# Two-layer gated attention block: the second layer's query projection, groups 2 to 6, by seven block products in place of eight

## The chip, the cores and the metric

The kernel runs on one core of a Trainium2 chip. The metric is the device time of one execution in microseconds (us), as the median of several runs of the same kernel. The engines are TensorE (PE: matmuls; PEld: its weight loads), VectorE (DVE), ScalarE (ACT), GpSimd (POOL) and SyncE (SP, which here only issues transfers). Each engine works through its own list of instructions in order, and the lists are tied together by semaphores.

## What is computed

The input is 16 sequences of 64 tokens with 512 features (1024 tokens in all), a context of the same shape, and two layers. Each layer is a gated attention over the context followed by a gated feed-forward part. The change touches the attention of the second layer alone, in the reference's own words:

```python
def _L1_xattn_ref(hidden_states, cross_attention_states, attention_mask, Wq, Wk, Wv, Wo, q_norm_w, k_norm_w):
    H, KVH, HD = (32, 8, 128)
    q = (hidden_states @ Wq.T).reshape(bsz, q_len, H, HD).transpose(0, 2, 1, 3)
    k = (cross_attention_states @ Wk.T).reshape(bsz, kv_len, KVH, HD).transpose(0, 2, 1, 3)
    v = (cross_attention_states @ Wv.T).reshape(bsz, kv_len, KVH, HD).transpose(0, 2, 1, 3)
    q = _rmsnorm(q, q_norm_w)
    k = _rmsnorm(jnp.repeat(k, GROUPS, axis=1), k_norm_w)
    scores = jnp.einsum('bhqd,bhkd->bhqk', q, k) * scale + attention_mask
    probs = jax.nn.softmax(scores.astype(jnp.float32), axis=-1)
    out = jnp.einsum('bhqk,bhkd->bhqd', probs, jnp.repeat(v, GROUPS, axis=1))
    return out.transpose(0, 2, 1, 3).reshape(bsz, q_len, H * HD) @ Wo.T
```

Everything is float32. A product of two float32 matrices is made of three passes on TensorE (`three`, L224): each operand is split into a high part of a shorter type (`_hi`, made by ScalarE) and the rest (`_lo`, made by a subtraction), and high x high, high x low and low x high are summed.

## The kernel before

The 32 query heads form 8 groups of 4 heads (J = 4); a group shares one key and value head. The 1024 tokens are cut into two halves of 512 (HALF). A unit u = 2g + h is one group g on one half h. The attention runs in steps, one for each unit, by a list written out by hand for each engine (`att_steps`, L881): groups 0, 1 and 7 are written out, groups 2 to 6 are a loop. Step (g, h) does three things at a time, for three units: the query projection of unit u, the scores and the softmax of unit u - 1, and values and output projection of unit u - 2.

TensorE's part of a step of the second layer (`step` in `att_pe`, L1022): the 16 small score matmuls of unit u - 1 (`score`, L966), which wait for the folded squares of its queries; the sums of squares for the norm (`folded_sums`, L947); `values` of unit u - 2 (L982), which waits for both parts of the probabilities (`p_hi`, `p_lo`) and for the last output addition of unit u - 3 (`y_added`), since it writes the same banks; then four heads of `project` (L924), 12 matmuls of 512 columns each, and four tiles of `project_out` (L1010), 12 matmuls of 512 columns each. The first `project` waits for `ssq_t`, that is until VectorE has read the sums out of PSUM; the score matmuls of the next step wait until VectorE has read the scores (`s_turned`).

VectorE's part (`step` in `att_dve`, L1532), in its order: `turn_sums` (L1439: two transposes out of PSUM, then eight copies of 32x16 elements, L1457, which end in `ssq_all`), `turn_scores` (L1432), `scale_scores` (L1473), the mask (L791), `maxima` (L1488 to L1496), two `out_low` (L1514: low parts of the values' output), `fold_squares` (L1463) for two heads, two `out_low`, `sums` (L1500, ends in `p_rec`), two `add_output` (L1521: adds a tile of the output projection to x), `turn_probs` (L1508), `fold_squares` for the other two heads, `att_probs_low` (L808: p_lo), two `add_output`.

GpSimd's part (`step` in `att_pool`, L1319): `att_shift` (L797, subtracts the maxima), `att_normalise` (L803), the low parts of the output weights (`wo_low`, L1310, four in a step h = 0) and of the next group's query weights (`att_wq_low`, L743, four in a step h = 1). In a step h = 0 the second, third and fourth `wo_low` are held back until `ssq_all`:

```python
                    for j in wo if do_finish and h == 0 and not (isinstance(g, int) and g == 1) else ():
                        if lay and j == 1:
                            pool.wait_ge(*c("ssq_all", us + 1))
                        wo_low(g - 1, j)
```

ScalarE squares and copies each head of queries out of PSUM (`queries`, L1144), makes the high parts, the exponentials and the norm factors (`norms`, L1155, from `ssq_all`). SyncE loads weights a group ahead. In group 1 the step (1, 0) is special (`second_opening`): VectorE does the shift itself there.

## Time and profile before

| | us |
|---|---|
| median of 3 runs | 1179.5 (1179.32 to 1179.86) |
| time of the profiled execution | 1179.01 |
| its span, first to last instruction | 1177.1 |
| one step of the loop of the second layer | 26.07 |
| second layer's attention, first scores to the last query step | about 746 to 1102 |

The page gives for each engine the busy share of the span, then the span in slices, the chain that ended last, and the costliest groups of instructions. Matmuls are pipelined: the duration of one is longer than the distance to the next, so TensorE's price is read from the distances between starts in the timeline, and not from the durations. On the other engines a duration includes the time in which an instruction has started but is held up.

### The profile page before, as it was taken

How to read it: one execution, taken by the hardware profiler on the slowest of the kernel's cores; microseconds unless marked ns; L12 is line 12 of the kernel's file. 1: busy time of each engine (PE TensorE's matmuls, PEld its weight loads, DVE VectorE, ACT ScalarE, POOL GpSimd, SP SyncE). 2: the span in 40 equal slices, each digit the busy share in tenths (PEclk: the TensorE clock that was granted, in tenths of full speed). 3: DMA queues.
4: the chain of work that ended last, by engine and by line, in shares of the span. 5: the costliest groups of instructions: out<-in, count | busy, mean ns of one | idle time of the engine just before them, and what ended most of it. 6: DMA issues, size and time to landing. Idle time of an engine off the chain costs nothing.

```text
span 1177.1 us, 17132 instructions
## 1 busy us (share of the span) xinstructions
PE 1169.5 (99%) x6272; PEld 946.7 (80%) x6272; DVE 880.9 (75%) x1538; ACT 424.0 (36%) x748; POOL 532.9 (45%) x371
## 2 busy tenths in 40 slices
PE   9999999999999999999999999999999999999998
PEld 8888888888788888777788888777777777777776
DVE  4656646898888888889984335798888887888695
ACT  5145152322322222231552123535453443435542
POOL 5522533766667676677463112305242433425410
PEclk9999999999999999999999999999999999999999
DMA  7944735812211221211210003121221221121101
GB/s 286 285 137 159 211 111 162 287 55 81 81 66 59 89 80 45 80 45 45 99 64 36 1 1 107 55 94 57 91 80 45 80 80 54 71 89 39 43 1 72
DMA packets 57315, 106.54 MB, mean 91 GB/s; under 512 B 3633, under 2 KB 36529, under 8 KB 51889
## 3 DMA queue, kind: packets, MB, share of 16 engines
q1 hardware_dynamic: 56736, 104.82, 26.0%
q0 software_dynamic: 384, 1.05, 0.2%
q8 instruction: 32, 0.52, 0.2%
q14 instruction: 19, 0.15, 0.0%
q10 hardware_dynamic: 144, 0.00, 0.0%
HBM read 78.59 MB, written 27.26 MB: 90 GB/s over the span
## 4 chain that ended last, share of the span: by engine, by line
PE 96%; DVE 2%; issue 0%; ACT 0%; DVEq 0%; POOL 0%; POOLq 0%
PE ps_q L226 14%; PE ps_b L226 14%; PE ps_b L228 14%; PE ps_b L227 14%; PE ps_q L227 13%; PE ps_q L228 13%; PE ps_s L978 5%; PE ps_b L1005 4%; PE ps_s L278 1%; PE ps_q L953 1%; PE ps_q L2152 1%; PE ps_b L479 1%; PE ps_s L1847 1%; PE ps_q L529 0%; PE ps_b L529 0%
## 5 line engine op out<-in xcount | busy, mean ns | idle before, releaser
L226 PE MATMUL ps_q<-hT_hi,wq_hi 128*128 128x512 f32 x512 | 203.2, 397 | 0.0
L227 PE MATMUL ps_q<-hT_lo,wq_hi 128*128 128x512 f32 x512 | 199.6, 390 | 0.0
L228 PE MATMUL ps_q<-hT_hi,wq_lo 128*128 128x512 f32 x512 | 199.2, 389 | 0.0
L226 PE MATMUL ps_b<-wo_hi,o_hi 128*128 128x512 f32 x440 | 171.6, 390 | 0.0
L227 PE MATMUL ps_b<-wo_lo,o_hi 128*128 128x512 f32 x440 | 171.2, 389 | 0.0
L228 PE MATMUL ps_b<-wo_hi,o_lo 128*128 128x512 f32 x440 | 171.2, 389 | 0.0
L743 POOL TENSOR_TENSOR wq_lo<-wq_raw,wq_hi 128x512 fp32r<-128x512 f32 x64 | 90.2, 1413 | 112.8 <-ACT wq_hi L737 112.8
L1317 POOL TENSOR_TENSOR qT<-q_t 128x512 f32<-128x512 f32 x64 | 89.8, 1405 | 66.3 <-DVE q_t L1430 60.8
L226 PEld LDWEIGHTS ps_q<-hT_hi,wq_hi 128*128 128x128 f32 x512 | 96.1, 188 | 24.3 <-issue 1.5
L228 PEld LDWEIGHTS ps_q<-hT_hi,wq_lo 128*128 128x128 f32 x512 | 96.1, 188 | 20.3
L227 PEld LDWEIGHTS ps_q<-hT_lo,wq_hi 128*128 128x128 f32 x512 | 96.2, 188 | 18.7
L1310 POOL TENSOR_TENSOR wo_lo<-wo_raw,wo_hi 128x512 fp32r<-128x512 f32 x56 | 83.5, 1507 | 56.4 <-ACT wo_hi L1142 38.3
L1184 ACT ACTIVATE p_hi<-pT 128x1024 fp32r<-128x1024 f32 x32 | 34.0, 1061 | 189.7 <-DVE pT L1512 189.7
L226 PEld LDWEIGHTS ps_b<-wo_hi,o_hi 128*128 128x128 f32 x440 | 82.6, 188 | 18.4 <-issue 1.4
L228 PEld LDWEIGHTS ps_b<-wo_hi,o_lo 128*128 128x128 f32 x440 | 82.6, 188 | 17.1
L227 PEld LDWEIGHTS ps_b<-wo_lo,o_hi 128*128 128x128 f32 x440 | 82.6, 188 | 17.1
L1529 DVE SCALAR_TENSOR_TENSOR x_sb<-ps_b,gates,x_sb 128x512 f32<-128x512 f32 x115 | 81.4, 722 | 18.0 <-PE ps_b L228 17.5
L803 POOL TENSOR_TENSOR p_sb<-p_sb,p_rec 128x1024 f32<-128x1024 f32 x29 | 55.7, 1920 | 83.8 <-DVE p_rec L1506 83.8
L1518 DVE TENSOR_TENSOR o_lo<-ps_b,o_hi 128x512 fp32r<-128x512 f32 x128 | 81.8, 682 | 12.6 <-ACT o_hi L1191 10.7
L1191 ACT ACTIVATE o_hi<-ps_b 128x512 fp32r<-128x512 f32 x128 | 66.5, 607 | 34.0 <-PE ps_b L1005 26.7
L1177 ACT ACTIVATE p_sb<-s_sb,zero_b 128x1024 f32<-128x1024 f32 x32 | 37.2, 1162 | 96.9 <-POOL s_sb L797 93.5
L797 POOL TENSOR_TENSOR s_sb<-s_sb,mx_c 128x1024 f32<-128x1024 f32 x28 | 53.8, 1921 | 32.1 <-DVE mx_c L1485 32.1
(301 smaller groups left out, 2498.0 us busy)
## 6 DMA issues: line engine op xcount, KB each, us to landing
wq_raw<-in_wq SPq DMA_DIRECT2D x16, 1024.0 KB, 4.8
...
```

The source lines that it names most:

```text
L226: nc.tensor.matmul(dst, l_hi, r_hi, start=first, stop=False)
L227: nc.tensor.matmul(dst, l_hi, r_lo, start=False, stop=False)
L228: return nc.tensor.matmul(dst, l_lo, r_hi, start=False, stop=last)
L743: nc.gpsimd.tensor_tensor(wq_lo[:, :, j * D:(j + 1) * D], wq_raw[:, :, j * D:(j + 1) * D], wq_hi[:, :, j * D:(j + 1) * D].bitcast(F32), AL ...
L797: eng.tensor_tensor(sc, sc, wide(mx_c[:, :], QB), ALU.subtract).then_inc(c["s_shifted"], 1)
L803: eng.tensor_tensor(pr, pr, wide(p_rec[:, :], QB), ALU.mult).then_inc(c["p_normed"], 1)
L978: last = nc.tensor.matmul(ps_s[par * S:(par + 1) * S, t * JS:(t + 1) * JS], kT[:, h, b:b + S], qT[:, h, :, b:b + S], start=True, stop=True)
L1191: nc.scalar.activation(o_hi[:, 2 * half:2 * half + 2, :, par * S:(par + 1) * S], ps_b[n].rearrange("p (t j q) -> p t j q", t=2, j=J), ACT. ...
L1310: nc.gpsimd.tensor_tensor(lo, wo_raw[:, j, :], hi.bitcast(F32), ALU.subtract).then_inc(c["wo_lo"], 1)
L1317: nc.gpsimd.tensor_tensor(qT[:, h, j, :], q_t1[:, j % 2, :], q_t2[:, j % 2, :], ALU.add).then_inc(c["q_rot"], 1)
L1518: nc.vector.tensor_tensor(o_lo[part], ps_b[n].rearrange("p (t j q) -> p t j q", t=2, j=J), o_hi[part].bitcast(F32), ALU.subtract).then_inc ...
L1529: nc.vector.scalar_tensor_tensor(x_sb[:, i, :], out_bank(u, t)[:, :], gates[:, lay:lay + 1], x_sb[:, i, :], ALU.mult, ALU.add).then_inc(c[ ...
```

## The change

For groups 2 to 6 of the second layer (ten units) the query projection of a unit, a product of a weight block of 512 features by 512 outputs with 512 tokens, is taken as a 2x2 by 2x2 product of blocks of 256 and made of seven block products in place of eight (the Strassen form of Winograd). A block product is 12 matmuls of 256 columns (2 output heads, 2 feature tiles, 3 passes), so a unit's projection is 84 matmuls of 256 columns in place of 48 of 512.

- The mixed token blocks t1 to t4 are made once for all groups by GpSimd, in the steps (0, 1), (1, 0) and (1, 1), with high parts by ScalarE and low parts by GpSimd: six instructions of 128x1024 after `lora_center` in (0, 1) and at the start of (1, 0), two after `att_normalise` in (1, 0), two at the start of (1, 1), four low parts.
- The mixed weight blocks s1 to s4 are made for each group by GpSimd (four sums of 128x512); each group then needs seven high parts (ScalarE) and seven low parts (GpSimd) of 128x512 in place of four and four. Six of the seven low parts stand behind `att_normalise` of the step h = 1; the four `wo_low` of the next step follow them, with no wait for `ssq_all`.
- Partial products that serve two outputs are joined by VectorE (four additions of 128x512 with one operand in PSUM for each unit), by two copies on ScalarE and by one addition on GpSimd. TensorE waits in between for two copies (`copied`) and for a join (`joined`), and its third product waits for `s_turned` as it writes the bank of the scores.
- `fold_squares` becomes two instructions of 64x1024 in place of four of 64x512. `turn_sums` stays as it is: VectorE still copies the sums of squares. The factor `qk_w` moves from the query copies to the staging of the keys, and its load to the start. Group 6 is written out after the loop, buffers are placed anew, some semaphore increments are dropped, and the scratch of software DMAs is set to 2048.

```diff
-                                 ACT.Copy).then_inc(c["k_staged1"], 1)
+                                 ACT.Copy, scale=qk_w[:, 0:1]).then_inc(c["k_staged1"], 1)
...
+        def woven(lay, g):
+            return lay == 1 and not (isinstance(g, int) and g in (0, 1, G - 1))
+        def builds_woven(lay, g, next_wq):
+            return lay == 1 and next_wq and not (isinstance(g, int) and g in (0, G - 2))
...
+        WOVEN_PARTS = ("a11", "s2", "s3", "a12", "a22", "s1", "s4")
...
+        def woven_low(pool, gt, name):
+            c = att[1]
+            pool.wait_ge(*c("woven_hi", 7 * (gt - 2) + WOVEN_PARTS.index(name) + 1))
+            f, hi, lo = woven_parts(name)
+            nc.gpsimd.tensor_tensor(lo, f, hi.bitcast(F32), ALU.subtract).then_inc(c["woven_lo"], 1)
...
+                l, r = woven_parts("s1")[0], woven_parts("a11")[0]
...
+                l, r = woven_parts("a22")[0], s2_f[:, :, :]
...
+                l, r = woven_parts("a12")[0], s2_f[:, :, :]
+            nc.gpsimd.tensor_tensor(out, l, r, ALU.subtract).then_inc(c["s_f"], 1)
...
+                    for q in range(2):
+                        for k in range(2):
+                            col = slice(q * D, (q + 1) * D)
+                            dst, closes = bank[:, q * QT:(q + 1) * QT], last_one and (q, k) == (1, 1)
+                            nc.tensor.matmul(dst, l_hi[:, k, col], r_hi[:, k, :], start=first and (q, k) == (0, 0), stop=False, skip_group_check=True)
+                            nc.tensor.matmul(dst, l_hi[:, k, col], r_lo[:, k, :], start=False, stop=False, skip_group_check=True)
+                            last = nc.tensor.matmul(dst, l_lo[:, k, col], r_hi[:, k, :], start=False, stop=closes, skip_group_check=True)
+                    return last
...
+                pe.wait_ge(*c("ssq_t", u))
+                if h == 0:
+                    pe.wait_ge(*c("t_hi", 4))
+                    pe.wait_ge(*c("t_lo", 4))
+                product(ps_q[0], "a11", tokens(0, 0), True).then_inc(c["product"], 1)
+                product(ps_q[1], "s2", mixed(t2_hi, t2_lo), True, True).then_inc(c["product"], 1)
+                pe.wait_ge(*c("s_turned", u))
+                product(ps_h[0], "s3", mixed(t3_hi, t3_lo), True).then_inc(c["product"], 1)
+                pe.wait_ge(*c("copied", 2 * n + 1))
+                product(ps_q[0], "a12", tokens(1, 0), False, True).then_inc(c["q_done"], 1)
+                product(ps_h[1], "s1", mixed(t1_hi, t1_lo), True).then_inc(c["q_done"], 1)
+                pe.wait_ge(*c("joined", 4 * n + 2))
+                product(ps_h[0], "a22", mixed(t4_hi, t4_lo), False, True).then_inc(c["q_done"], 1)
+                pe.wait_ge(*c("copied", 2 * n + 2))
+                product(ps_h[1], "s4", tokens(1, 1), False, True).then_inc(c["q_done"], 1)
...
+            def woven_step(g, h, next_wq):
...
+                norms(us)
+                act.wait_ge(*c("product", 3 * n + 1))
+                act.wait_ge(*c("scored", u - 1))
+                nc.scalar.activation(qT[:, h, 0:2, late], heads(ps_q[0]), ACT.Copy).then_inc(c["copied"], 1)
+                out_high(up, 0)
+                out_high(up, 1)
+                if building:
+                    woven_high(act, g + 1, "a11")
+                out_high(up, 2)
+                out_high(up, 3)
+                if building:
+                    woven_high(act, g + 1, "s2")
+                act.wait_ge(*c("q_done", 4 * u + 1))
+                act.wait_ge(*c("ssq", u))
+                nc.scalar.activation(q_sq[:, 0:2, early], heads(ps_q[0]), ACT.Square).then_inc(c["q_sq"], 1)
+                nc.scalar.activation(qT[:, h, 0:2, early], heads(ps_q[0]), ACT.Copy).then_inc(c["q_rot"], J)
+                act.wait_ge(*c("q_done", 4 * u + 2))
+                nc.scalar.activation(q_sq[:, 2:4, late], heads(ps_h[1]), ACT.Copy).then_inc(c["copied"], 1)
+                if building:
+                    woven_high(act, g + 1, "s3")
+                exponentials(us)
+                act.wait_ge(*c("joined", 4 * n + 3))
+                square(slice(2, 4), early)
+                if building:
+                    woven_high(act, g + 1, "a12")
+                elif next_wq:
+                    att_wq_high(act, lay, g + 1, 0)
+                act.wait_ge(*c("joined", 4 * n + 4))
+                square(slice(0, 2), late)
+                act.wait_ge(*c("c22_made", n + 1))
+                square(slice(2, 4), late)
+                if building:
+                    woven_high(act, g + 1, "a22")
+                    woven_high(act, g + 1, "s1")
+                    woven_high(act, g + 1, "s4")
+                elif next_wq:
+                    for j in range(1, J):
+                        att_wq_high(act, lay, g + 1, j)
+                probs_high(us)
...
+                if second_opening(lay, g, h):
+                    mixed_high(t1_hi, t1_f, 3)
+                    mixed_high(t2_hi, t2_f, 8)
...
+            def mixed_first(f, t, l, r):
+                pool.wait_ge(*lns[2]("lo", NT))
+                nc.gpsimd.tensor_tensor(by_half(f), quarters(hT_hi, *l), quarters(hT_hi, *r), ALU.subtract).then_inc(c["t_f"], 1)
+                nc.gpsimd.tensor_tensor(by_half(t), quarters(hT_lo, *l), quarters(hT_lo, *r), ALU.subtract).then_inc(c["t_f"], 1)
+            def mixed_joined(f, t, turn):
+                pool.wait_ge(*c("t_f", turn - 1))
+                nc.gpsimd.tensor_tensor(f[:, :, :], f[:, :, :], t[:, :, :], ALU.add).then_inc(c["t_f"], 1)
+            def mixed_next(f, l, r, turn, before):
+                pool.wait_ge(*c("t_f", before))
+                nc.gpsimd.tensor_tensor(by_half(f), quarters(hT_hi, *l), by_half(r), ALU.subtract).then_inc(c["t_f"], 1)
+                pool.wait_ge(*c("t_f", turn - 1))
+                nc.gpsimd.tensor_tensor(by_half(f), by_half(f), quarters(hT_lo, *l), ALU.add).then_inc(c["t_f"], 1)
+            def mixed_low(lo, hi, f, turn):
+                pool.wait_ge(*c("t_hi", turn))
+                nc.gpsimd.tensor_tensor(lo[:, :, :], f[:, :, :], hi[:, :, :].bitcast(F32), ALU.subtract).then_inc(c["t_lo"], 1)
...
+            def woven_step(g, h, next_wq):
...
+                if h == 0:
+                    for j in range(J):
+                        wo_low(g - 1, j)
+                elif building:
+                    woven_sum(pool, g + 1, "s2")
+                    woven_sum(pool, g + 1, "s3")
+                    woven_low(pool, g + 1, "a11")
+                att_shift(pool, lay, u - 1)
+                pool.wait_ge(*c("copied", 2 * n + 2))
+                pool.wait_ge(*c("joined", 4 * n + 2))
+                nc.gpsimd.tensor_tensor(qT[:, h, 2:4, late], qT[:, h, 2:4, late], q_sq[:, 2:4, late], ALU.add).then_inc(c["c22_made"], 1)
+                if h and building:
+                    woven_sum(pool, g + 1, "s4")
+                elif next_wq:
+                    att_wq_low(pool, lay, g + 1, 0)
+                att_normalise(pool, lay, u - 1)
+                if h == 0 and not (isinstance(g, int) and g == G - 2):
+                    woven_sum_first(pool, g + 1)
+                elif building:
+                    for name in WOVEN_PARTS[1:]:
+                        woven_low(pool, g + 1, name)
+                elif next_wq:
+                    for j in range(1, J):
+                        att_wq_low(pool, lay, g + 1, j)
...
+                if second_opening(lay, g, h):
+                    mixed_joined(t3_f, t3_t, 6)
+                    att_normalise(pool, lay, us)
+                    mixed_next(t2_f, (1, 1), t1_f, 8, 3)
+                    woven_sum_first(pool, 2)
+                    woven_sum(pool, 2, "s2")
+                    woven_sum(pool, 2, "s3")
+                    woven_sum(pool, 2, "s4")
+                    mixed_low(t1_lo, t1_hi, t1_f, 1)
+                    return
+                if builds_woven(lay, g, next_wq):
+                    mixed_next(t4_f, (1, 0), t2_f, 10, 8)
+                    att_shift(pool, lay, us)
+                    mixed_low(t2_lo, t2_hi, t2_f, 2)
+                    woven_low(pool, 2, "a11")
+                    woven_low(pool, 2, "s2")
+                    att_normalise(pool, lay, us)
+                    woven_low(pool, 2, "s3")
+                    woven_low(pool, 2, "a12")
+                    mixed_low(t3_lo, t3_hi, t3_f, 3)
+                    woven_low(pool, 2, "a22")
+                    woven_low(pool, 2, "s1")
+                    mixed_low(t4_lo, t4_hi, t4_f, 4)
+                    woven_low(pool, 2, "s4")
...
+                    mixed_first(t1_f, t1_t, (0, 1), (0, 0))
+                    mixed_joined(t1_f, t1_t, 3)
+                    mixed_first(t3_f, t3_t, (1, 1), (0, 1))
...
+                dve.wait_ge(*c("q_sq", 4 * u + 2 * r + 2))
+                nc.vector.tensor_tensor(q_sq[own, :, tok], q_sq[own, :, tok], q_sq[other, :, tok], ALU.add).then_inc(c["q_fold"], 2)
...
+            def woven_step(g, h):
...
+                turn_sums(us, 1 - h)
+                turn_scores(us, 1 - h)
+                scale_scores(us)
+                dve.wait_ge(*c("copied", 2 * n + 1))
+                dve.wait_ge(*c("product", 3 * n + 2))
+                joined(part_b, ps_q[1], part_b).then_inc(c["joined"], 1)
+                att_mask(dve, lay, us, 1 - h)
+                dve.wait_ge(*c("joined", 4 * n + 1))
+                dve.wait_ge(*c("product", 3 * n + 3))
+                joined(part_d, ps_h[0], part_b).then_inc(c["joined"], 1)
+                maxima(us)
+                out_low(up, 0)
+                out_low(up, 1)
+                dve.wait_ge(*c("q_done", 4 * u + 3))
+                joined(qT[:, h, 2:4, early], ps_h[0], part_b).then_inc(c["joined"], 1)
+                out_low(up, 2)
+                dve.wait_ge(*c("q_done", 4 * u + 4))
+                joined(part_b, ps_h[1], part_b).then_inc(c["joined"], 1)
+                out_low(up, 3)
+                sums(us)
+                add_output(up, h, 0)
+                fold_woven(u, 0)
+                turn_probs(us)
+                fold_woven(u, 1)
+                att_probs_low(dve, lay, us)
+                for t in range(1, PAIRS):
+                    add_output(up, h, t)
...
```

## Rows read from the trace of the kernel before

**Rows 1.** The page: busy time of the engines; the chain that ended last, by engine.
```profile
PE 1169.5 (99%) x6272; PEld 946.7 (80%) x6272; DVE 880.9 (75%) x1538; ACT 424.0 (36%) x748; POOL 532.9 (45%) x371
...
PE 96%; DVE 2%; issue 0%; ACT 0%; DVEq 0%; POOL 0%; POOLq 0%
```
**Rows 2.** Timeline of TensorE, one step: start us, us, engine, line, what.
```profile
866.09 1.95 PE L978 MATMUL ps_s<-qT,kT 128*64 128x256 f32 x16
867.97 0.66 PE L953 MATMUL ps_q<-q_sq,ones 64*32 64x256 f32 x16
...
870.51 0.40 PE L227 MATMUL ps_q<-hT_lo,wq_hi 128*128 128x512 f32 x1
...
881.19 0.39 PE L226 MATMUL ps_b<-wo_hi,o_hi 128*128 128x512 f32 x1
...
892.16 1.95 PE L978 MATMUL ps_s<-qT,kT 128*64 128x256 f32 x16
```
**Rows 3.** Timelines of TensorE and of its weight loads: shorter matmuls elsewhere.
```profile
650.47 0.36 PE L227 MATMUL ps_b<-uT_lo,hT_hi 128*128 128x448 f32 x1
...
651.89 0.36 PE L228 MATMUL ps_b<-uT_hi,hT_lo 128*128 128x448 f32 x1
...
1152.35 1.75 PEld L2152 LDWEIGHTS ps_q<-a_raw,xT 128*128 128x128 f32 x15
```
**Rows 4.** Timeline of VectorE, the same step as rows 2.
```profile
869.64 1.43 DVE L1457 COPY r_s<-r_t 32x16 f32<-32x16 f32 x8
871.10 1.25 DVE L1435 STREAM_TRANSPOSE s_sb<-ps_s 128x1024 f32<-128x1024 f32 x1
872.45 1.23 DVE L1479 TENSOR_TENSOR s_sb<-s_sb,r_q 128x1024 f32<-128x1024 f32 x1
873.71 2.20 DVE L791 TENSOR_TENSOR s_sb<-s_sb,mask_sb 128x1024 f32<-128x1024 f32 x1
...
884.63 0.35 DVE L1506 RECIPROCAL p_rec<-sm_c 128x32 f32<-128x32 f32 x1
...
892.27 0.75 DVE L1529 SCALAR_TENSOR_TENSOR x_sb<-ps_b,gates,x_sb 128x512 f32<-128x512 f32 x1 [0.18 <-PE ps_b L228]
```
**Rows 5.** Timeline of GpSimd, the same step.
```profile
871.23 3.60 POOL L1310 TENSOR_TENSOR wo_lo<-wo_raw,wo_hi 128x512 fp32r<-128x512 f32 x2 [3.04 <-DVE r_s L1457]
...
885.06 1.92 POOL L803 TENSOR_TENSOR p_sb<-p_sb,p_rec 128x1024 f32<-128x1024 f32 x1 [5.08 <-DVE p_rec L1506]
```
**Rows 6.** Busy time by stretch, of step (1, 0); the first line names the columns.
```profile
core 0: us, PE busy (x) PEld busy (x) DVE busy (x) ACT busy (x) POOL busy (x), PEclk, DMA share, GB/s
761.30:787.70 26.40, 25.73 (x140) 20.39 (x137) 24.07 (x40) 10.65 (x19) 3.97 (x3) 1.00 0.23 90
```
**Rows 7.** VectorE's small instructions beside GpSimd: timelines at 747 and 280 us.
```profile
747.41 1.14 DVE L1457 COPY r_s<-r_t 32x16 f32<-32x16 f32 x2
747.07 1.27 POOL L1310 TENSOR_TENSOR wo_lo<-wo_raw,wo_hi 128x512 fp32r<-128x512 f32 x1 [2.38 <-ACT wo_hi L1142]
...
280.74 1.38 DVE L1485 TENSOR_TENSOR mx_c<-mx_a 32x32 f32<-32x32 f32 x2
280.79 1.29 POOL L1310 TENSOR_TENSOR wo_lo<-wo_raw,wo_hi 128x512 fp32r<-128x512 f32 x1
```
**Rows 8.** One line each, all its instructions: duration ns min/median/max.
```profile
L1457 DVE COPY r_s<-r_t x120: 161/167/946, 747.4 to 1103.9; 32x16 f32<-32x16 f32 x120
...
L1518 DVE TENSOR_TENSOR o_lo<-ps_b,o_hi x40: 678/686/694, 799.9 to 1038.4; 128x512 fp32r<-128x512 f32 x40
```
**Rows 9.** Timeline of VectorE and TensorE from step (1, 0) to (1, 1).
```profile
765.71 1.95 DVE L1457 COPY r_s<-r_t 32x16 f32<-32x16 f32 x8
...
773.32 1.29 DVE L1518 TENSOR_TENSOR o_lo<-ps_b,o_hi 128x512 fp32r<-128x512 f32 x2 [0.66 <-ACT o_hi L1191]
...
786.20 1.41 DVE L1470 TENSOR_TENSOR q_sq<-q_sq 64x512 f32<-64x512 f32 x2
...
787.71 1.95 PE L978 MATMUL ps_s<-qT,kT 128*64 128x256 f32 x16 [0.68 <-issue]
```

217 lines of the change are left out of this document (184 added, 33 removed).

## The prediction

> **What bounds the kernel now.** I read the page first: TensorE is busy 99% of the span and the chain that ended last lies on it for 96% [rows 1]. So the time is TensorE's own list, and each microsecond that its list gets shorter or longer is a microsecond of the kernel. Then the timeline of one step of the loop [rows 2]: the scores start at 866.09 and those of the next step at 892.16, so a step takes 26.07 us with no hole in it. From 870.51 to 881.19 lie 47 projection matmuls of 512 columns: 10.68/47 = 0.227 us from one to the next (durations of 0.39 overlap). Then VectorE in the same step [rows 4], since the change gives it work: it starts on the sums once they are there, at 868.63, that is T+2.5 (T is the start of the scores, 866.09) [rows 2], and its last instruction ends at 893.02, that is T+26.9, or 0.9 into the next step. It has to be clear of that by T+2.5 of the next step, where `values` writes the banks and the next sums are ready. So VectorE has some 1.6 us to spare in a step. GpSimd is busy for 4 of 26.4 us in the first such step [rows 6] and looks free.
>
> It is not free beside VectorE, and this decides the case. While GpSimd works on one `wo_low` after another, the scaling of the scores (872.45, 1.23 us) goes through, but the `wo_low` beside it stretches: two of them take 3.60 us where one takes 1.28 [rows 5, 7]. The mask behind it, the same size and also with both operands in SBUF, takes 2.20 instead of 1.23 [rows 4]. They exclude each other: each holds up the other for a whole instruction, and they take turns. Even the smallest are held: one copy of the sums has a median of 167 ns but a maximum of 946 [rows 8], and that one stands beside a `wo_low` (two copies in 1.14 us at 747.41) [rows 7]. At 280.74 two VectorE instructions of 180 ns take 1.38: the first passes, the second waits for GpSimd's whole instruction [rows 7]. Instructions that read PSUM are not held: `out_low`, one operand in PSUM, has a maximum of 694 over a median of 686, often with GpSimd busy beside it [rows 8]. The kernel before keeps clear of this where it hurts: GpSimd waits 3.04 us for the eighth copy before it goes on with `wo_low` [rows 5].
>
> The Trainium skill, page "SBUF — State Buffer", section "Who interferes with whom", says the same and speaks against the change: a VectorE instruction with two SBUF inputs contends with GpSimd's, a copy in a two-port mode does too, and whoever is first has the shared ports for its whole instruction. The trace agrees (2.20 against 1.23 us, 946 against 167 ns). By that rule the step below in which copies and GpSimd take turns holds, and the rival in which they don't falls.
>
> **The change on TensorE.** Per unit it removes 48 x 0.227 = 10.90 us and adds 84 matmuls of 256 columns. No full-height one of 256 columns is in the trace. The bounds: matmuls of 448 columns lie 1.42/7 = 0.203 us apart [rows 3], so 64 columns cost 0.024, and a straight line gives 0.227 - 4 x 0.024 = 0.131; by the 2.4 GHz level (clock 1.00 [rows 6]) 256 columns fewer are 0.107 less, 0.120. Weight loads of 128 columns follow each other every 1.56/14 = 0.111 us [rows 3], below that, so they stay hidden; if they did not, the sum of both, 0.23, would be the end. I take 0.121, from the clock. Saved: 10.90 - 84 x 0.121 = 0.73 a unit, 7.3 us in ten.
>
> The same skill's page "TensorE: Matmul & The Clock Gate", section "Back-to-back issue gap", gives N/2.4 + 2.5 ns for a matmul of N columns alone: 215.8 and 109.2 ns, and by it the saving would be 10.36 - 9.17 = 1.2 us a unit. The trace has 227 ns where the page has 216.
>
> **The change on VectorE and GpSimd.** VectorE gets four joins of 0.69 (the price of `out_low`, also one PSUM operand [rows 8]), + 2.5 us a unit as they start 0.62 apart. Four folds of 0.7 (1.41 for two [rows 9]) become two of 64x1024, for which I take the mask's 1.23 without wait [rows 4], - 0.3. GpSimd gets nine more instructions of 1.29 in a group (three low parts, four sums, two additions), 11.6 us. Prices: 1.29 for 128x512, 1.92 for 128x1024 [rows 5, 7]. I now walk through a group with these prices and the turn-taking.
>
> Second half (h = 1), T at its scores: copies T+3.4 to 4.8, scores read by 6.1, scaled by 7.3, first join 8.1; the mask waits for the s2 sum on GpSimd and ends at 9.8; maxima 12.8 (held 0.4 by a low part), two `out_low` by 14.1. TensorE's seven products, 1.45 us each from T+4.3, end at 14.4: no wait. `p_rec` at 18.9. Then GpSimd: normalise to 20.9, and six low parts and, from the next step, four `wo_low`, ten instructions 1.25 apart. VectorE's two folds and p_lo push in between, each waiting up to 1 us: folds 22.0 and 25.5, p_lo 27.7, and three output additions to 29.8. TensorE is done at T+25.5. GpSimd is done at 20.9 + 12.5 + 3 x 0.95 = 36.3.
>
> First half of the next group (h = 0), T at its scores, 25.5 later: VectorE comes free at 4.3 in place of 0.9, so `values` starts at 4.3 in place of 2.5 (1.8 lost), and the sums are transposed by 5.0. GpSimd has back-to-back work until 36.3 - 25.5 = 10.8. So one copy of 0.17 us passes between each two GpSimd instructions: 5.7, 6.9, 8.2, 9.4, and the other four from 10.7 to 11.4. The scores are read out by 12.7. TensorE's third product, which writes that bank, was due at 7.1 and starts at 12.7: 5.6 us lost in all. After it come four more products and the output projection, 5 x 1.45 + 10.97: the step ends at 30.9 against 26.07. GpSimd has little left to do by then, so the tail is free of waits: p_lo at 31.3, the additions at 33.4, that is T+2.5 of the next step, just in time.
>
> So groups 3 to 6: first half + 4.9 (four times, 19.5); second halves 25.5, - 0.55 (five times, - 2.8).
>
> Entry, step (1, 0) (T = 761.26, where T of the next is 26.45 later [rows 9]): GpSimd's six 128x1024 instructions run from T+5.7, while VectorE has done four of its eight copies. The other four each wait for one: 11.5 in place of 6.4. p_lo 14.4, scaling 17.3, mask 20.2, each behind another of them, so the two `out_low` end at 21.5 in place of 13.35 (774.61) [rows 9], and the output projection, due at 14.6, starts at 21.5. `p_rec` is at 29.7; after normalise (31.7) the two t2 instructions take turns with the folds, which end at 36.5 in place of 26.35 (787.61) [rows 9]. The next scores wait for them, as they already do today (0.68 us idle [rows 9]): + 10.0.
>
> Step (1, 1): ScalarE makes the high part of t2 before p_hi, so p_lo comes at T+3.5 and the additions at 4.9: `values` is 2.4 late. Copies take turns with s4, t1's low part and t4 (six us instead of 1.4), the two `out_low` are 2.0 late for the output projection, and the folds, behind low parts, end 3.4 after TensorE: + 7.8.
>
> First half of group 2: seven GpSimd instructions are left at the copies; the third product starts at T+13.2 in place of 7.1. It ends at 31.4: + 5.3.
>
> Sum: 10.0 + 7.8 + 5.3 + 19.5 - 2.8 = + 39.8 (TensorE's 7.3 saved is in it). The profiled execution is 1179.0 (1177.1 and 1.9 around); 1218.8, and as the median stands 0.5 above it, 1219.
>
> Edits priced at nothing: ScalarE's three more high parts a group (0.6 each; it is busy for 10.7 of 26.4 us [rows 6]); the key staging's factor (same instruction); the earlier load and the dropped increments. If the smaller DMA scratch slows the gathers at the start, it is some us, in no row.
>
> **The rivals.**
> - VectorE is served first when both ask. For it: the scaling at 872.45 went before a `wo_low` of 872.48. Against: the mask waited its turn. The walk then loses 3.3 us in a pair of steps less (27.8 for a first half), and less at the entry: + 20, 1199.
> - The small copies slip through together once GpSimd pauses. For: eight copies with one wait took 1.95 at 765.71 [rows 9]. Against: at 280.74 the second was held [rows 7], and GpSimd has no pause here. A first half then loses only 1.8 by late additions: 27.2, entry + 7 and + 5: + 14, 1193.
> - Heavier: joins are held too, or GpSimd's strided 128x1024 take 2.2: + 45, 1224.
> - The other side: the extra GpSimd work waits instead of VectorE, and TensorE stays the bound with - 7.3, of which the t2 chain before p_hi in (1, 1) gives back 3.3: 1175. It decides for faster if VectorE's waits stay under its 1.6 us to spare a step; the walk has 4 to 7. Against it: 946 ns for a copy of 167.
> - The block products cost 0.131 or show their weight loads: at 0.131, + 8.4 us of TensorE, part of it inside the waits, 1224; at 0.23, 84 x 0.11 x 10 = + 90.
>
> **Chances.** Forecast 0.50; VectorE first 0.15; copies pass 0.11; heavier 0.10; dearer matmuls 0.04; faster 0.07; about equal, by a mix of small waits, 0.03. The range that leaves out the last two and some of the dear end is 1190 to 1228. A measurement of this kernel can tell 0.2%, 2.4 us, from no change. Faster 0.07, within it 0.03, slower 0.90.
>
> **What the profile after would show.** The eight copies in a step h = 0 as one group of 6 to 7 us in place of 1.43; TensorE idle for about 3.7 us before the third product, released by VectorE's transposition of the scores; first halves of 31, second halves of 25.5; durations over 2 us for folds and p_lo; (1, 0) of 36 us. TensorE's matmuls of 256 columns 0.121 apart tell the price. The prediction is wrong if the copies stay at 1.4 us with GpSimd's instructions stretched instead, or if the chain stays on TensorE without holes.

## The result, and the profile after

The kernel after takes 1234.15 us (median of 5 runs, 1231.15 to 1235.16), the kernel before 1179.44 in the same session: 1.046 times as long, with a 95% interval from 1.0445 to 1.0474. The forecast was 1219 with a range up to 1228. The direction and most of the mechanism came out as worked out; the size did not, by 15 us, and the time lies outside the range.

The profiled execution has a span of 1233.3 us, 56.2 more than before. Its page: busy time of the engines, TensorE's busy share and granted clock in 40 slices, and the chain that ended last, by engine and by line:

```profile
PE 1178.6 (96%) x6632; PEld 968.6 (79%) x6632; DVE 965.7 (78%) x1558; ACT 429.0 (35%) x757; POOL 640.3 (52%) x430
...
PE   9999999999999999999999999687989898989998
...
PEclk9999999999999999999999999998999999999999
...
PE 19%; DVE 13%; issue 4%; POOL 1%; ACT 0%; DVEq 0%; ACTq 0%
DVE r_s L1777 3%; PE ps_b L252 3%; PE ps_b L254 3%; PE ps_b L253 3%; PE ps_s L1138 1%; PE ps_b L1165 1%; DVE o_lo L1845 1%; PE ps_s L1086 1%; DVE x_sb L1856 1%; DVE q_sq L1798 1%; PE ps_s L1088 1%; PE ps_s L1087 1%; PE ps_q L252 1%; DVE q_s
```

VectorE has 85 us more busy time than in [rows 1], of which 27 are the 40 joins. The chain no longer lies on TensorE for 96%: its share is 19% and VectorE's 13% (the shares printed add up to 37% only), and the copies of the sums (L1777) stand first in its list. TensorE's busy share is still 96%; its idle stretches, called holes here, show only as lower digits in the second half of the slices. The steps show them better. Busy time by stretch, steps (1, 0), (1, 1), (2, 0), (2, 1), (3, 0), (3, 1), each from one score to the next (columns as in [rows 6]: length, then busy time and instructions of TensorE, its weight loads, VectorE, ScalarE and GpSimd, then the clock and the DMA share and rate):

```profile
764.18:801.98 37.80, 27.77 (x140) 21.60 (x137) 36.06 (x39) 10.83 (x19) 26.57 (x12) 0.95 0.17 63
801.98:838.53 36.55, 28.34 (x152) 21.37 (x153) 33.50 (x39) 17.70 (x31) 28.42 (x16) 0.95 0.11 37
838.53:872.28 33.75, 28.97 (x188) 24.29 (x188) 31.05 (x41) 8.69 (x15) 18.98 (x12) 0.85 0.20 71
872.28:897.90 25.62, 25.44 (x189) 21.67 (x189) 23.95 (x40) 12.45 (x23) 15.85 (x10) 1.00 0.15 53
897.90:930.24 32.34, 26.97 (x188) 23.24 (x188) 30.73 (x42) 10.70 (x19) 17.89 (x12) 0.95 0.21 73
930.24:955.86 25.62, 25.39 (x189) 21.67 (x189) 23.94 (x40) 12.50 (x23) 15.87 (x10) 1.00 0.15 51
```

Three more pairs like the last follow (the last second half takes 25.13). The clock column is the one to look at: 1.00 in the second halves and below 1.00 wherever a step is long. The sums, in us against the kernel before (26.07 a step; 26.45 for (1, 0) [rows 9], 26.23 for (1, 1), 27.07 for (7, 0)):

| | forecast | measured | length |
|---|---|---|---|
| up to the first scores of the layer | 0 | + 2.9 | 749.4 |
| (1, 0) | + 10.0 | + 11.4 | 37.80 |
| (1, 1) | + 7.8 | + 10.3 | 36.55 |
| (2, 0) | + 5.3 | + 7.7 | 33.75 |
| four first halves, groups 3 to 6 | + 19.5 | + 25.1 | 32.3 each |
| five second halves | - 2.8 | - 2.9 | 25.6 to 25.1 |
| (7, 0), not woven | 0 | + 1.7 | 28.8 |
| sum | + 39.8 | + 56.2 | |

The first half (3, 0) line by line, with T = 897.90 at its scores. VectorE, timeline:

```profile
897.70 2.19 DVE L923 TENSOR_TENSOR p_lo<-pT,p_hi 128x1024 fp32r<-128x1024 f32 x1
899.82 2.06 DVE L1856 SCALAR_TENSOR_TENSOR x_sb<-ps_b,gates,x_sb 128x512 f32<-128x512 f32 x3
...
902.68 6.35 DVE L1777 COPY r_s<-r_t 32x16 f32<-32x16 f32 x8
909.06 1.25 DVE L1755 STREAM_TRANSPOSE s_sb<-ps_s 128x1024 f32<-128x1024 f32 x1
910.41 1.23 DVE L1806 TENSOR_TENSOR s_sb<-s_sb,r_q 128x1024 f32<-128x1024 f32 x1
```

GpSimd beside it, and then TensorE:

```profile
893.07 3.53 POOL L820 TENSOR_TENSOR s_lo<-s_f,s_hi 128x512 fp32r<-128x512 f32 x2
896.55 5.70 POOL L820 TENSOR_TENSOR wq_lo<-wq_raw,wq_hi 128x512 fp32r<-128x512 f32 x3
902.22 1.29 POOL L820 TENSOR_TENSOR s_lo<-s_f,s_hi 128x512 fp32r<-128x512 f32 x1
903.47 4.99 POOL L1546 TENSOR_TENSOR wo_lo<-wo_raw,wo_hi 128x512 fp32r<-128x512 f32 x4
```

```profile
901.92 0.39 PE L1165 MATMUL ps_b<-p_hi,v_hi 64*128 64x256 f32 x2 [1.48 <-DVE x_sb L1856]
...
906.26 0.28 PE L1087 MATMUL ps_q<-t_lo,s_hi 128*128 128x256 f32 x1
906.38 0.28 PE L1088 MATMUL ps_q<-t_hi,s_lo 128*128 128x256 f32 x1
910.55 0.36 PE L1086 MATMUL ps_s<-t_hi,s_hi 128*128 128x256 f32 x1 [3.88 <-DVE s_sb L1755]
...
911.49 0.41 PE L1086 MATMUL ps_s<-t_hi,s_hi 128*128 128x256 f32 x1
911.71 0.41 PE L1087 MATMUL ps_s<-t_lo,s_hi 128*128 128x256 f32 x1
...
914.26 0.41 PE L1087 MATMUL ps_q<-hT_lo,wq_hi 128*128 128x256 f32 x1
```

The eight copies take 6.35 us in place of 1.43 [rows 4]: one is let through after each GpSimd instruction until the fourth `wo_low` ends at 908.46, that is T+10.6 (10.8 in the walk). TensorE waits 1.48 us for the additions before `values` and 3.88 us for the scores before the third product, which starts at T+12.65 (12.7). Then comes what the walk did not have: from 911.3 to 914.5 the matmuls of 256 columns start 0.213 us apart, after 0.12 before the hole. That is the lower of TensorE's two clock levels (half clock below), for 16 matmuls: 16 x 0.095 = 1.5 us. (The Trainium skill, page "TensorE: Matmul & The Clock Gate", section "Back-to-back issue gap", has N/1.2 for this level, 213.3 ns; the trace agrees with 213 to 214.)

### The profile page after: what moved, and what is told of

Its sections match the earlier page's. It is cut to its first block and busy times, and to the rows that moved or that the text cites. A ratio compares the mean times of both kernels' runs of the same rounds, so it can differ in the third digit from the quotient of the medians.

```text
span 1233.3 us, 18035 instructions
## 1 busy us (share of the span) xinstructions
PE 1178.6 (96%) x6632; PEld 968.6 (79%) x6632; DVE 965.7 (78%) x1558; ACT 429.0 (35%) x757; POOL 640.3 (52%) x430
## 5 line engine op out<-in xcount | busy, mean ns | idle before, releaser
L252 PE MATMUL ps_q<-hT_hi,wq_hi 128*128 128x512 f32 x352 | 140.2, 398 | 3.1 <-ACT qT L1318 3.0
L253 PE MATMUL ps_q<-hT_lo,wq_hi 128*128 128x512 f32 x352 | 137.2, 390 | 0.0
L254 PE MATMUL ps_q<-hT_hi,wq_lo 128*128 128x512 f32 x352 | 137.0, 389 | 0.0
L252 PEld LDWEIGHTS ps_q<-hT_hi,wq_hi 128*128 128x128 f32 x352 | 66.1, 188 | 21.0 <-ACT qT L1318 3.5
L1546 POOL TENSOR_TENSOR wo_lo<-wo_raw,wo_hi 128x512 fp32r<-128x512 f32 x56 | 74.9, 1357 | 13.9 <-ACT wo_hi L1307 10.8
L254 PEld LDWEIGHTS ps_q<-hT_hi,wq_lo 128*128 128x128 f32 x352 | 66.1, 188 | 14.0
L253 PEld LDWEIGHTS ps_q<-hT_lo,wq_hi 128*128 128x128 f32 x352 | 66.2, 188 | 12.8
L854 POOL TENSOR_TENSOR wq_lo<-wq_raw,wq_hi 128x512 fp32r<-128x512 f32 x44 | 66.2, 1512 | 18.7 <-ACT wq_hi L768 18.7
```

The costliest lines, as they stand in the source:

```text
L252: nc.tensor.matmul(dst, l_hi, r_hi, start=first, stop=False)
L253: nc.tensor.matmul(dst, l_hi, r_lo, start=False, stop=False)
L254: return nc.tensor.matmul(dst, l_lo, r_hi, start=False, stop=last)
L854: nc.gpsimd.tensor_tensor(wq_lo[:, :, j * D:(j + 1) * D], wq_raw[:, :, j * D:(j + 1) * D], wq_hi[:, :, j * D:(j + 1) * D].bitcast(F32), AL ...
L1546: nc.gpsimd.tensor_tensor(lo, wo_raw[:, j, :], hi.bitcast(F32), ALU.subtract).then_inc(c["wo_lo"], 1)
```

## The experiments

All times are medians; the kernel before had 1178.9 to 1179.2 us in these sessions. The theory: GpSimd's and VectorE's instructions exclude each other, what this holds up becomes holes of TensorE, and each long hole costs a stretch at half clock besides. The rivals: TensorE's smaller matmuls, VectorE's additional joins, the order of ScalarE, and a plain shortage of VectorE time.

**The copies on ScalarE.** In all steps from (1, 0) to (7, 0):

```
+                sums_by_quadrant(us)
                 norms(us)
...
+                if not (isinstance(u, int) and u == 0):
+                    return
                 dve.wait_ge(*c("ssq_t", u + 1))
-                if not (isinstance(u, int) and u == 0):
-                    dve.wait_ge(*c("r_ln", u))
```

(The first part is ScalarE's list, the second ends VectorE's `turn_sums` ahead of its copies.)

> The eight copies of the sums go from VectorE to ScalarE in all steps from (1, 0) to (7, 0). Theory (the copies take turns with GpSimd, and what they hold up is the time): the scores of a first half are read out by T+6.5 in place of T+12.4, the hole of 4.2 us before the third product goes, and with it the stretch at half clock behind it; first halves of groups 3 to 6 go from 32.3 to about 27.4 us (the late additions still hold up the values by 1.9), (2, 0) from 33.8 to 27.5, (1, 0) and (1, 1) lose 3 to 5 us each, second halves stay at 25.6. Sum about -34 us, 1200 us (1194 to 1208). Rival (VectorE's whole load, the folds and p_lo held by GpSimd, is what counts, and the copies only stand where VectorE would wait anyway): first halves stay above 30.5 and the time above 1222.

Measured: 1200.56 us (1.0185, interval 1.0168 to 1.0202). First halves of groups 3 to 6 take 26.7, (2, 0) 27.0, (1, 0) 37.0, (1, 1) 34.1. The first halves and (2, 0) came out 0.5 to 0.7 better than expected; (1, 0) gained only 0.8 and (1, 1) 2.5 (3 to 5 each expected). Taking the copies off VectorE gives back 34 of the 55 us; that also takes 1.4 us of work a step from VectorE, which the next run leaves in place. Steps (2, 1) and (3, 0):

```profile
860.38:885.91 25.53, 25.32 (x189) 21.67 (x189) 23.05 (x33) 14.18 (x31) 15.77 (x10) 1.00 0.16 53
885.91:912.63 26.72, 25.22 (x188) 21.66 (x188) 24.77 (x34) 12.50 (x27) 19.92 (x12) 1.00 0.24 88
```

**GpSimd waits for the eighth copy.** The kernel before had such a wait, and the woven step dropped it:

```
                 if h == 0:
+                    pool.wait_ge(*c("ssq_all", u))
                     for j in range(J):
                         wo_low(g - 1, j)
```

> GpSimd waits for the eighth copy before the four low parts of the output weights in the first halves of groups 2 to 6; nothing else differs. Theory: only the low part that already runs at the first copy holds one up; the other seven pass in 1.3 us, and the scores are read out at about T+8.3 in place of T+12.4. First halves of groups 3 to 6 come to 27.3 to 28.0 us from 32.3, (2, 0) from 33.8 to some 30 (there low parts of the query weights stand at the copies, and they are not held back), the rest as it was: about -23 us, 1211 us (1206 to 1218). Rival (GpSimd's work is only moved and holds up the mask and the maxima behind the copies instead): first halves lose less than 2 us, above 1224 us.

Measured: 1208.56 us (1.0251, 1.0234 to 1.0268); first halves 27.5, (2, 0) 28.4. One wait brings back 25 us, and VectorE's work is the same, so that a plain shortage of VectorE time is not what made the first halves long. VectorE in (3, 0): eight copies with GpSimd held back

```profile
894.74 2.12 DVE L1778 COPY r_s<-r_t 32x16 f32<-32x16 f32 x8
896.89 1.25 DVE L1756 STREAM_TRANSPOSE s_sb<-ps_s 128x1024 f32<-128x1024 f32 x1
```

take 2.12 us, and only the first meets a low part. Since nothing else differs, neither the joins nor the smaller matmuls can be the cause of the large hole.

This run shows one thing more. In steps (1, 0) and (1, 1) the kernel after has holes of 3.71 and 4.19 us with half clock behind each. Here the hole before the values of (1, 0) is as long, 3.70, and the values behind it run at full clock (12 pairs 0.12 us apart); the scores of (1, 1) run at full clock too. Yet the two steps are as long as in the kernel after, 37.80 and 36.55:

```profile
775.61 0.39 PE L1165 MATMUL ps_b<-p_hi,v_hi 64*128 64x256 f32 x2 [3.70 <-issue]
...
761.59:799.40 37.81, 27.71 (x141) 21.54 (x137) 36.07 (x39) 10.72 (x19) 26.57 (x12) 0.95 0.17 63
799.40:835.92 36.52, 28.22 (x153) 22.07 (x153) 33.48 (x39) 17.68 (x31) 28.39 (x16) 0.94 0.11 36
```

The half clock comes later here, behind holes of 3.22 us before the output projection of (1, 0) and 2.40 before the values of (1, 1), and the hole at the end of (1, 0) is 3.18 us in place of 4.19. VectorE sets the length of the two steps (in (1, 0) it is busy for 36.06 of 37.80 us in the kernel after), and what TensorE loses or gains there only makes a later hole shorter or longer.

**That wait taken out of the kernel before.** The one part of the change alone:

```
-                        if lay and j == 1:
-                            pool.wait_ge(*c("ssq_all", us + 1))
```

> The kernel before without the one wait that the change drops: GpSimd's second low part of the output weights no longer waits for the eighth copy of the sums. Nothing else of the change is in it. Theory: two or three more copies are held up for 1.1 us each, the scores are read out up to 3 us later, but the projections of this kernel write other banks than the scores, so TensorE does not wait for that; VectorE has 1.6 us to spare at the end of a step: first halves stay within 0.3 us of 26.07, 1179 to 1181 us. Rival (any such hold-up reaches the end of the step, whatever the banks): first halves grow by 1.5 us and more, above 1187 us.

Measured: 1179.53 us (ratio 1.0002, 0.9992 to 1.0011): no change, all steps at 26.07. The trace shows the holds all the same:

```profile
870.21 3.40 DVE L1455 COPY r_s<-r_t 32x16 f32<-32x16 f32 x8
```

3.40 in place of 1.43 us. A hold costs only where TensorE waits for what stands behind it. In the kernel before the scores' banks are needed 26 us later; in the woven step the third product writes them 7 us after the scores.

**Less work for GpSimd.** In groups 3 to 6 the sums and their low parts on 8 columns, so most of them are left out:

```
+            cut = slice(None) if isinstance(gt, int) else slice(0, 8)
-            nc.gpsimd.tensor_tensor(out, l, r, ALU.subtract).then_inc(c["s_f"], 1)
+            nc.gpsimd.tensor_tensor(out[:, :, cut], l[:, :, cut], r[:, :, cut], ALU.subtract).then_inc(c["s_f"], 1)
```

> In groups 3 to 6 the seven additional GpSimd instructions of a group that make the sums of weight blocks and their low parts work on 8 columns of each row in place of 256 (so most of these sums and low parts are left out, and the output is another); ScalarE reads a plain block in place of the sums. Semaphores, order and TensorE's work are unchanged. Theory: without these 9 us of GpSimd the low parts are over sooner, the additions come before the values, and the copies meet at most two low parts of the output weights: first halves of groups 3 to 6 from 32.3 to 26.0 (25.5 to 27.5), second halves 25.5, the steps up to (2, 0) unchanged: about -25 us, 1209 us. Rival (the lost time is in VectorE's four joins or in TensorE's smaller matmuls): no first half falls by over 1.5 us, above 1227 us.

Measured: 1216.32 us (1.0316, 1.0299 to 1.0333), where 1209 was expected. First halves fall to 29.2, not 26.0: the copies still met three `wo_low`, the hole before the third product was still 2.0 us, and matmuls 0.213 apart followed it:

```profile
898.55 4.42 DVE L1783 COPY r_s<-r_t 32x16 f32<-32x16 f32 x8
```

The second halves, free of waits, take 25.13: 0.94 under 26.07, which is what TensorE gains by the seven products. The rival that the products or the joins cost the time falls.

**Work in the hole.** The second product three times over in first halves, 24 matmuls more each:

```
+                for _ in range(2 if h == 0 else 0):
+                    product(ps_q[1], "s2", mixed(t2_hi, t2_lo), True, True)
                 product(ps_q[1], "s2", mixed(t2_hi, t2_lo), True, True).then_inc(c["product"], 1)
```

> In the first halves of groups 2 to 6 TensorE makes the second product three times over (24 matmuls of 256 columns more, 2.9 us) before it goes on, and so works through most of the hole of 4.2 us in front of the third product. Theory (the half clock of some 3.4 us behind each hole is caused by the hole and costs 1.4 us each time): the hole shrinks to about 1.3 us, the matmuls behind it lie 0.12 apart at once, and first halves of groups 3 to 6 go from 32.3 to 30.9 us, (2, 0) from 33.8 to about 32; about -7 us, 1227 us, although TensorE has 14 us more work. Rival (the slow matmuls behind the hole come from something else, or the additional work delays the join of the second product): first halves stay at 32.3 or grow by up to 2.9 us, 1234 to 1249 us.

Measured: 1224.97 us (1.0389, 1.0372 to 1.0406): 9 us less with 120 matmuls more. First halves take 30.85, 1.5 less; (2, 0) 32.0. TensorE in (4, 0), and the stretch of that step:

```profile
965.31 0.36 PE L1086 MATMUL ps_s<-t_hi,s_hi 128*128 128x256 f32 x1 [1.12 <-DVE s_sb L1757]
...
966.09 0.28 PE L1086 MATMUL ps_s<-t_hi,s_hi 128*128 128x256 f32 x1
```

```profile
952.62:983.47 30.85, 28.25 (x212) 1.00 0.22 76
```

The third product starts at T+12.7 as in the kernel after, but the hole is 1.12 us, the clock of the step 1.00, and the matmuls lie 0.12 apart. So the half clock came from the hole, and it costs 1.5 us in each first half and 1.75 in (2, 0). The steps give 7.7 of the 9.2 us; the rest was not traced and lies within the scatter of 4 us between the runs of the kernel after.

**The entry without the mixing.** The ten GpSimd instructions that make t1 to t4 on 8 columns, so that most of the mixing is left out:

```
-                nc.gpsimd.tensor_tensor(by_half(f), quarters(hT_hi, *l), quarters(hT_hi, *r), ALU.subtract).then_inc(c["t_f"], 1)
+                nc.gpsimd.tensor_tensor(by_half(f)[:, :, :, 0:8], quarters(hT_hi, *l)[:, :, :, 0:8], quarters(hT_hi, *r)[:, :, :, 0:8], ALU.subtract).then_inc(c["t_f"], 1)
```

> The ten GpSimd instructions of steps (0, 1) to (1, 1) that mix the blocks of the hidden state (t1 to t4) work on 8 columns of each row in place of all (so most of the mixing is left out and the output is another; the high and low parts read a plain block). Theory (the entry is slow since GpSimd's ten instructions of 2.4 us, up to 3.4 beside VectorE, exclude VectorE's scaling, mask, folds and low parts): (1, 0) falls from 37.8 to about 27 us and its windows have a clock of 1.00, (1, 1) from 36.6 to about 30 (its low parts of t2 to t4 and of the seven weight blocks stay), (2, 0) from 33.8 to about 33, the rest is unchanged: -18 us, 1216 us (1211 to 1220). Rival (the entry waits for ScalarE's order, t1 and t2 before the high part of the probabilities, or for the projections): (1, 0) stays above 33 and the time above 1226.

Measured: 1216.21 us (1.0313, 1.0296 to 1.033). Steps (1, 0) and (1, 1):

```profile
761.22:788.88 27.66, 25.77 (x140) 20.43 (x137) 25.39 (x40) 12.24 (x20) 10.21 (x14) 1.00 0.23 86
788.88:818.81 29.93, 26.21 (x153) 20.88 (x153) 28.38 (x39) 16.65 (x29) 21.74 (x14) 1.00 0.14 45
```

27.7 and 29.9 us, as expected, with ScalarE's order as it was, so that order is not what holds up the entry; (2, 0) is 34.3 (33 expected). The mixing, 10 instructions in the whole kernel, costs some 16 us by the steps (18 by the medians, with the scatter of the start).

**GpSimd's instructions cut in two.** The same work in twice as many instructions:

```
+            for cut in (slice(0, D), slice(D, WD)):
+                last = nc.gpsimd.tensor_tensor(out[:, :, cut], l[:, :, cut], r[:, :, cut], op)
+            last.then_inc(sem, 1)
```

> The kernel after with GpSimd's sums and low parts of the weight blocks and its low parts of the output weights each cut into two instructions of 128x256; the same work, order and semaphores. Theory (one VectorE instruction passes between two GpSimd instructions, so a hold lasts as long as the GpSimd instruction that is running): a copy is held for about 0.65 us in place of 1.22, folds and p_lo take at most 1.9 in place of 2.5, the additions end 1 to 2 us sooner, the scores are read out at T+9 to T+10 in place of T+12.4; first halves of groups 3 to 6 fall from 32.3 to between 27.5 and 29, (2, 0) by 3: about -20 us, 1213 us (1208 to 1220). Rival (VectorE is held until GpSimd's queue runs dry, or cutting makes GpSimd's work longer by as much): first halves stay above 31.5, 1229 us and more.

Measured: 1218.57 us (1.0344, 1.0327 to 1.0361). First halves 30.1, then 29.0; (2, 0) 32.0, (1, 1) 34.5. The direction holds, the first halves gained a little less than expected. Steps (3, 0) and (4, 0), and the matmul behind the large hole of each:

```profile
891.41:921.53 30.12, 26.97 (x189) 23.20 (x188) 29.00 (x42) 10.85 (x19) 21.81 (x22) 0.94 0.22 78
947.17:976.20 29.03, 25.72 (x190) 21.72 (x189) 28.33 (x42) 10.74 (x19) 21.79 (x22) 1.00 0.23 81
...
901.84 0.55 PE L1092 MATMUL ps_s<-t_hi,s_hi 128*128 128x256 f32 x1 [2.99 <-DVE s_sb L1763]
...
957.57 0.36 PE L1092 MATMUL ps_s<-t_hi,s_hi 128*128 128x256 f32 x1 [3.00 <-DVE s_sb L1763]
```

The same hole, at T+10.4 in both, is followed by half clock in (3, 0) and not in (4, 0); the two steps, of the same instructions, differ by 1.1 us. The copies of one first half:

```profile
950.72 5.33 DVE L1785 COPY r_s<-r_t 32x16 f32<-32x16 f32 x8
```

The held ones take 0.67 or 0.68 us beside GpSimd instructions of 0.72 or 0.73, where they take 1.21 to 1.24 beside 1.26 to 1.29: a hold is as long as the GpSimd instruction that is under way, and one small instruction passes between two of them. (The Trainium skill, page "SBUF — State Buffer", section "Who interferes with whom", has an exclusive lock for the whole instruction; both lengths agree.)

**Low parts held until p_lo.** On top of the copies on ScalarE (1200.56):

```
                 elif building:
+                    pool.wait_ge(*c("p_lo", u))
                     for name in WOVEN_PARTS[1:]:
                         woven_low(pool, g + 1, name)
```

> As the kernel with the copies on ScalarE (1200.6 us), and in the second halves of groups 2 to 5 GpSimd waits for VectorE's low part of the probabilities before its six low parts of the weights. Theory (what is left in a first half, 26.7 us against 25.5, is the values waiting for VectorE's additions, since folds and p_lo of the step before take 2.2 to 2.5 us in place of 1.2 behind those low parts): folds and p_lo take 1.2 us, the additions end before the values are due, first halves of groups 3 to 6 come to 25.6 us, second halves stay at 25.5: about -5 us, 1196 us (1193 to 1199). Rival (the low parts come too late for the products that read them, or hold up the scaling and the mask instead): first halves do not fall, or grow by 1 to 3 us, 1200 to 1210 us.

Measured: 1209.78 us (1.0259, 1.0242 to 1.0276); the rival was right in the time, though it named the scaling and the mask. One fold is still held (2.48, by the normalisation), the second and p_lo take 1.22 and 1.23 and the additions are in time, but GpSimd's work now lies beside the maxima:

```profile
897.24 3.37 DVE L1818 TENSOR_TENSOR mx_c<-mx_a 32x32 f32<-32x32 f32 x4
900.63 0.69 DVE L1851 TENSOR_TENSOR o_lo<-ps_b,o_hi 128x512 fp32r<-128x512 f32 x1
```

Four instructions of 0.18 us take 3.37, the output projection waits 2.55 us for `o_lo` behind them, the half clock follows, and first halves take 29.3.

**out_low ahead of the maxima.** On top of that:

```
-                maxima(us)
                 out_low(up, 0)
                 out_low(up, 1)
+                maxima(us)
```

> As the kernel with held low parts (1209.8 us), and VectorE makes the first two low parts of the output blocks ahead of the maxima instead of behind them. Theory: in that kernel two of the four small maxima (0.18 us each) wait 1.2 us for a low part of the output weights, and so the output projection starts 2.8 us late and partly at half clock; with the order turned, o_lo is there at about T+11.5, the projection waits only for GpSimd's fourth low part (T+14.9, due at T+14.1), and first halves of groups 3 to 6 fall from 29.3 to 26.0 to 26.5, with second halves at 25.3: about -14 us, 1195 us (1192 to 1199). Rival (the later maxima hold up the probabilities and so the end of the step, or the low parts of the output weights are what is late): first halves stay above 28, 1204 us and more.

Measured: 1204.06 us (1.021, 1.0193 to 1.0227), 9 us worse than expected. First halves take 27.1, second halves 25.7; neither the theory (26.0 to 26.5) nor the rival (above 28) has that. Two waits stand where one was:

```profile
900.35 0.47 PE L252 MATMUL ps_b<-wo_hi,o_hi 128*128 128x512 f32 x1 [0.89 <-POOL wo_lo L1551]
912.01 1.95 PE L1138 MATMUL ps_s<-qT,kT 128*64 128x256 f32 x16 [0.55 <-DVE q_sq L1804]
```

The low parts of the output weights come late, and the later maxima bring the folds behind the end of the step; (6, 1) and (7, 0) lose 3.5 us more.

**Another order in the entry.** On top of that, in (1, 0) all `out_low` ahead of the maxima, in (1, 0) and (1, 1) both pairs of folds ahead of `sums`, and in ScalarE the high part of the probabilities ahead of those of t1 and t2:

```
+                        for n in range(4):
+                            out_low(up, n)
                         maxima(us)
```

> As the last one, and in the entry: in step (1, 0) all four low parts of the output blocks come ahead of the maxima, in (1, 0) and (1, 1) the second pair of folds comes ahead of the sums, and ScalarE makes the high parts of t1 and t2 behind those of the probabilities. Theory: the hole of 7 us before the output projection of (1, 0) goes (it waits for o_lo behind three small maxima that wait 2.1 us each), (1, 0) falls from 37.0 to about 32 us, (1, 1) from 34.1 to 32 to 34: -5 to -8 us against the last one, about 1189 us. Rival (VectorE and GpSimd together have more work at the shared ports than the two steps have time, whatever the order): the gain is under 2 us.

Measured: 1205.47 us (1.0221, 1.0204 to 1.0238). (1, 0) falls from 37.0 to 27.2, more than expected, and all of it comes back: (1, 1) takes 37.8 in place of 34.1 and (2, 0) 34.9 in place of 26.8. The wait before the values of (1, 1):

```profile
803.10 0.58 PE L1165 MATMUL ps_b<-p_hi,v_hi 64*128 64x256 f32 x2 [9.08 <-DVE x_sb L1862]
```

The rival held: this order moved the wait and did not remove it. In (1, 0) and (1, 1) of the kernel after GpSimd is busy for 55 of 74 us and VectorE for 70, waits for each other included.

**Both remedies.** Copies on ScalarE and instructions cut in two:

```
+                sums_by_quadrant(us)
+            in_halves(c["woven_lo"], lo, f, hi.bitcast(F32), ALU.subtract)
```

> The copies of the sums on ScalarE (1200.6 us so far) and GpSimd's sums and low parts of weights cut in halves (the kernel after with this alone: 1218.6 us). Theory (what is left of a first half with the copies on ScalarE, 26.7 us against 25.5, is folds and p_lo that wait for whole low parts, so that the additions end 1.2 us late): with waits of half the length first halves of groups 3 to 6 come to 25.6 to 26.2, (1, 1) from 34.1 to 32.5, (2, 0) from 27.0 to 26: about -5 us, 1196 us (1193 to 1199), the best of all with seven products, and still above the kernel before, by the entry. Rival (cut instructions give VectorE no time, since it now waits twice as often): within 1 us of 1200.6.

Measured: 1201.46 us (1.0189, 1.0172 to 1.0206), no gain over 1200.56. First halves take 26.5 and (1, 1) 30.7, 3.4 less, but the low parts of the mixed blocks are late for the first product of (2, 0), a step that takes 33.8 in place of 27.0. The two halves of a cut GpSimd instruction take 0.73 each, 1.46 together, in place of 1.29; whether this is what makes the low parts late was not tried apart. The wait before that product:

```profile
839.16 0.55 PE L1092 MATMUL ps_q<-hT_hi,wq_hi 128*128 128x256 f32 x1 [5.56 <-POOL t_lo L1589]
```

**The smaller DMA scratch alone**, in the kernel before:

```
-    nc = bacc.Bacc("TRN2", target_bir_lowering=False, num_devices=1)
+    nc = bacc.Bacc("TRN2", target_bir_lowering=False, num_devices=1, dynamic_dma_scratch_size=2048)
```

> The kernel before, with nothing of the change but the smaller DMA scratch. The first 10 us differ between the profiles so far: the first matmul on loaded data starts at 5.03 us in the kernel before and at 5.26 to 6.43 in five kernels with the change, with a stretch at half clock behind it. Theory (that is when the first loads land in a given run, not the scratch): the time is that of the kernel before, 1178.5 to 1180 us, with a first matmul anywhere between 5.0 and 6.5. Rival (the scratch delays the loads): the first matmul at 5.3 or later and 1 to 3 us more in all rounds, 1180 to 1182 us.

Measured: 1179.19 us (1.0001, 0.9991 to 1.0011), so the scratch is not what costs time. In its profile the first matmuls on loaded data start at 4.92 us and lie 0.43 apart until about 6.8, as at half clock; the clock column has 1.00 there and does not agree:

```profile
4.92 1.19 PE L529 MATMUL ps_q<-kw_hi,cT_hi 128*128 128x512 f32 x2
...
7.89 0.61 PE L529 MATMUL ps_q<-kw_hi,cT_lo 128*128 128x512 f32 x2
```

In the kernel after the first block of `c_raw` was there at 5.85 in place of 4.44 us, that matmul started at 6.43, and the wide spacing lasted until 10. In the ten experiments with the change the second layer's scores begin between 0.1 us earlier and 3.0 us later than in the kernel before. Why the loads land later in some runs was not tried; it is part of the scatter of 4 us between the runs of the kernel after.

## Why the prediction was off

**What held.** TensorE stays the bound where no wait comes in. The mechanism (GpSimd and VectorE take turns, and the copies of the sums wait) and its place in the step came out. So did these sizes: second halves of 25.6 us (25.5 forecast); 0.118 to 0.121 us for a matmul of 256 columns with its weight load hidden (0.121); joins of 0.68, not held beside GpSimd; the copies until T+11.1 (11.4) and the third product at T+12.65 (12.7) in a first half; the output projection of (1, 0) at T+21.9 (21.5); the third product of (2, 0) at T+13.6 (13.2). VectorE was not served first, and the copies did not slip through together: those two rivals fall by the 6.35 us, and with them the one in which GpSimd waits.

**What failed: the step from a hole to its price.** In "First half of the next group" the prediction adds the idle time of 5.6 us and then runs "four more products and the output projection" at full clock. Behind the hole of 3.9 us TensorE ran at half clock for 16 matmuls. In a first half that is 1.5 us (32.34 against 30.85 with the hole filled), four times 6; in (2, 0), where a hole of 4.69 stands before the third product, 20 matmuls at 0.213 are 1.9, of which the filled hole gave back 1.75. Together this is 7.7 us, against 16.4 missing in the profiled execution, and the run with work in the hole shows it. No rival had it, since all were worked out at full clock.

Half clock also follows the holes before the values of (1, 0) (3.71 us) and before the scores of (1, 1) (4.19; 16 matmuls in 3.57 in place of 1.95 us). There it did not set the length: in the kernel in which GpSimd waits these values and scores run at full clock, the half clock lies elsewhere in the steps, and they take 37.81 and 36.52 in place of 37.80 and 36.55. Behind a hole of 4.40 the scores of (2, 0) are slow too, 16 matmuls in 2.84 in place of 1.95; with the hole before the third product filled they stay so, and their cost was not tried apart.

**A price taken from the wrong row.** The prediction took 1.92 us for GpSimd's instructions of 128x1024, from the normalisation [rows 5]. Its second operand is only 128x32, repeated along the row. With two whole operands such an instruction takes 2.4, in the kernel before as well (duration in ns, min/median/max):

```profile
L808 POOL TENSOR_TENSOR p_lo<-pT,p_hi x13: 2382/2397/3464, 243.2 to 550.6; 128x1024 fp32r<-128x1024 f32 x13
...
L803 POOL TENSOR_TENSOR p_sb<-p_sb,p_rec x29: 1913/1920/1924, 208.8 to 1118.8; 128x1024 f32<-128x1024 f32 x29
```

The mixing took 2.34 to 2.41, and up to 3.38 beside VectorE; the rival "heavier" had 2.2. The folds of (1, 0) ended at T+37.7 (36.5 forecast), and in (1, 1) the eight copies took 8.1 us (six forecast). As VectorE sets the length of both steps, this fits the 1.4 and 2.5 us missing there; it is argued from the rows, and no run has the price alone changed.

**Smaller misses.** In (1, 1) ScalarE's copies of the queries stand behind `norms`, which waits for the eight copies, so that the second projection waited 3.04 us for `qT`: a queue that the walk had not passed through, though VectorE's folds end later still and hide it (where GpSimd waits, this wait is 1.51 and the step 36.52). (7, 0) was taken as unchanged; its values wait 1.65 us for late additions like those of the first halves, and it takes 28.8 in place of 27.1. The start, + 2.9 us, is of that execution: other runs of woven kernels had between 0 and 3.

**The range.** It was built from rivals that differ in who waits for whom, each at full clock, and its upper end of 1228 lies below the fastest run, 1231.15. The forecast of 1219 and the 7.7 us of half clock make 1227, still inside it; only with the 3.9 us missing in (1, 0) and (1, 1) as well is it 1231.
